# Four attention stages on one core: balanced seats for masked outputs, first heads' rows stored ahead, constants issued later, fills in two halves

## What is computed

```python
x = x + masked_attention(ln(x))    # 16 heads of 8; softmax over keys k >= query q
x = x + ffn0(ln(x))                # one of 8 weight matrices, chosen by argmax
x = x + radial_attention(ln(x))    # exp(-sigma * |q - k|^2), no softmax
x = x + ffn0(ln(x))
x = x + relative_attention(ln(x))  # scores with a shifted relative term, softmax
x = x + ffn1(ln(x))
x = x + rotary_attention(ln(x))    # rotary positions on q and k, softmax
x = x + ffn1(ln(x))
```

## Time and profile before

| | us |
|---|---|
| median of 3 runs | 2823.63 |
| lowest, highest | 2823.32, 2838.18 |
| the profiled execution | 2820.36 |
| its span in the trace | 2818.6 |
| PE busy in it | 2662.6 (94%) |
| ACT busy | 2103.6 (75%) |
| DVE busy | 2070.0 (73%) |
| POOL busy | 898.3 (32%) |

### The profile page before, as it was taken

How to read it: one execution, slowest core, us unless ns; L and a number is a source line. 1 busy time by engine, 2 the same in 40 slices (tenths; PEclk the granted TensorE clock), 3 DMA queues, 4 the chain that set the end, 5 groups by cost and what they waited for, 6 DMA issues and landing times.

```text
span 2818.6 us, 107129 instructions
## 1 busy us (share of the span) xinstructions
PE 2662.6 (94%) x43752; PEld 1600.2 (57%) x43752; DVE 2070.0 (73%) x5519; ACT 2103.6 (75%) x3769; POOL 898.3 (32%) x1604
## 2 busy tenths in 40 slices
PE   5999999999999999999999999999999999999996
PEld 3666665655555555666666666666644444444444
DVE  6788888722222228888788888878889989999993
ACT  3677776799999996666666666666677878878874
POOL 2212223321303242622541361252135144351321
PEclk7999999999999999999999999999999999999998
DMA  3534232433423342411321241222123123232221
GB/s 113 152 100 118 81 115 80 116 119 113 127 88 121 104 147 57 133 53 57 93 88 50 73 131 50 74 81 70 46 64 107 56 71 98 66 98 68 68 72 32
DMA packets 197218, 250.16 MB, mean 89 GB/s; under 512 B 48292, under 2 KB 113124, under 8 KB 196728
## 3 DMA queue, kind: packets, MB, share of 16 engines
q1 hardware_dynamic: 195288, 241.21, 28.9%
q10 hardware_dynamic: 1440, 2.10, 0.2%
HBM read 132.89 MB, written 100.07 MB: 83 GB/s over the span
## 4 chain that ended last, share of the span: by engine, by line
PE 69%; DVE 20%; issue 5%; ACT 2%; DMA 1%; SPq 1%; POOL 0%; ACTq 0%; DVEq 0%; POOLq 0%
PE ppv L1010 29%; DVE mx L1311 14%; PE ring L867 6%; PE ring L917 6%; PE ring L852 5%; PE ring L878 4%; PE ring L950 3%; PE pm L1050 2%; DVE seen L1295 2%; DVE seen L1306 1%; ACT probs L1167 1%; PE ring L966 1%; PE pm L1035 1%; PE pm L1113 1%; PE pm L1104 1%
## 5 line engine op out<-in xcount | busy, mean ns | idle before, releaser
L1167 ACT ACTIVATE probs<-ring 128x512 f32<-128x512 f32 (+1 forms) x3280 | 1970.1, 682 | 647.0 <-PE ring L867 316.0
L1311 DVE TENSOR_REDUCE mx<-ring 128x1 f32<-128x512 f32 (+2 forms) x2112 | 1284.9, 651 | 226.6 <-PE ring L917 89.3
L1010 PE MATMUL ppv<-probs,values 128*32 128x128 f32 x30208 | 1147.3, 278 | 7.5 <-POOL probs L1590 3.1
L1010 PEld LDWEIGHTS ppv<-probs,values 128*32 128x32 f32 x30208 | 793.1, 109 | 320.1 <-issue 162.9
L1306 DVE CUSTOM_DVE_ANT_0 seen<-ring,low_seen 128x512 f32<-128x512 f32 x576 | 392.9, 682 | 71.8 <-PE ring L917 71.5
L924 PE MATMUL ring<-kst,qst 48*128 48x512 bf16 (+1 forms) x1060 | 361.6, 390 | 34.8 <-DMA kst<-records_k 17.4
L878 PE MATMUL ring<-qst,kst 51*128 51x512 bf16 (+2 forms) x1092 | 345.5, 384 | 4.5 <-ACT probs L1167 3.6
L1560 POOL CAST mparts<-mall 128x8 bf16<-128x8 f32 x192 | 37.0, 193 | 827.6 <-DVE mall L1329 700.8
L917 PE MATMUL ring<-kst,qst 112*128 112x512 bf16 (+3 forms) x768 | 251.5, 328 | 11.8 <-DVE mx L1295 6.7
L1590 POOL TENSOR_SCALAR_AFFINE_SELECT probs<-probs 128x512 f32<-128x512 f32 x128 | 81.6, 638 | 564.0 <-ACT probs L1167 351.3
L867 PE MATMUL ring<-qst,kst 115*128 115x512 bf16 (+3 forms) x768 | 250.9, 327 | 0.0
(11 more groups left out here) (170 smaller groups left out, 3001.9 us busy)
## 6 DMA issues: line engine op xcount, KB each, us to landing
qst<-records_q SPq DMA_DIRECT2D x448, 96.0 KB
heads_out<-osb SPq DMA_DIRECT2D x256, 128.0 KB, 2.0
kst<-records_k SPq DMA_DIRECT2D x320, 96.0 KB
records_k<-parts SPq DMA_DIRECT2D x96, 256.0 KB, 3.2
records_q<-parts SPq DMA_DIRECT2D x90, 256.0 KB, 3.4
kst<-records_k SPq DMA_DIRECT2D x128, 102.0 KB
oT<-heads_out SPq DMA_DIRECT2D x60, 128.0 KB, 2.7
proj<-proj SPq DMA_DIRECT2D x96, 64.0 KB, 2.0
```

What stands on the lines that cost most here:

```text
L1010: mm = pe.matmul(ppv[32 * g:32 * g + 32, c:c + P], values[:, (n // H) % 2, v:v + 32], src[:, at * P:(at + 1) * P], start=u == 0 and qt < 4 ...
L1167: nc.scalar.activation(probs_of(rd.n, u), src, ACT.Exp, scale=1.0 if rd.s == RBF else SCALE).then_inc(s_exp, 1)
L1311: ins = dve.tensor_reduce(mx[:, slot, to:to + 1], bank[:, at * P:(at + nt) * P], AX.X, ALU.max)
```

## The change

It has four parts.

1. **Seats.** A function `seat` gives each query tile its column tile. In the masked stage the tiles 4 to 7 are seated in reverse order, 3 to 0, instead of 0 to 3. In `KQ_UNITS[MASKED]` the single tiles (4, 4) and (0, 0) change places between units 3 and 8. The output projection reads `oT` by the same function.
2. **First heads ahead.** The rows of the first `EARLY = 4` heads are stored first, on a semaphore of their own (`s_r0`), and head 0's load waits for these only. The rows of the other 12 are stored by SP after the loads of heads 0 to 2, and by ACT after the small operations of the operator choice.
3. **Constants.** Fourteen constants move to ACT's queue, behind the arrival of the first rows of `x`. SP's `others()` begins in round 3 instead of 1 and issues one transfer every four ticks instead of two; the constants of the last two stages come last and have a semaphore `s_c2`, which PE, ACT, DVE and POOL wait for before round `REL_WORK` = 96, in the middle of the radial stage. The memset of `values` moves from DVE to POOL. SP's rows of ones of the radial stage are issued one by one in `others()`.
4. **Halves.** Where fills are 6 ticks apart (radial and rotary intervals, but not the last radial one), a fill other than `nm` and `zs` is cut in two: the second half (`rest`) is due one tick after the first, and the copy (`take`) and what follows from it one tick later than before. A fill of 512 columns becomes two matmuls of 256 columns, one of four matmuls or transposes becomes two and two.

```diff
+EARLY = 4
 KQ_UNITS = {
-    MASKED: [[(7, 0, 4, 0)], [(7, 4, 4, 0)], [(6, 0, 4, 0)], [(6, 4, 3, 0), (4, 4, 1, 3)], [(5, 0, 4, 0)],
-             [(5, 4, 2, 0), (1, 0, 2, 2)], [(4, 0, 4, 0)], [(3, 0, 4, 0)], [(2, 0, 3, 0), (0, 0, 1, 3)]],
+    MASKED: [[(7, 0, 4, 0)], [(7, 4, 4, 0)], [(6, 0, 4, 0)], [(6, 4, 3, 0), (0, 0, 1, 3)], [(5, 0, 4, 0)],
+             [(5, 4, 2, 0), (1, 0, 2, 2)], [(4, 0, 4, 0)], [(3, 0, 4, 0)], [(2, 0, 3, 0), (4, 4, 1, 3)]],
...
+def seat(s, qt):
+    g = 3 - qt % 4 if s == MASKED and qt >= 4 else qt % 4
+    return g, qt // 4 * P
...
         self.at[("fill", *name)] = tick
-        self.at[("take", *name)] = tick + 1
+        last = tick + (self.apart > 3 and name[2] not in ("nm", "zs"))
+        self.at[("rest", *name)] = last
+        self.at[("take", *name)] = last + 1
         self.free = tick + self.apart
-        return tick + 1
+        return last + 1
...
+        NC_ACT = 16 * 14
+        REL_WORK = (REL * B - 2) * H
...
-                if n % H == 0:
+                if n == 0:
+                    sp.wait_ge(s_r0, 16 * STORES[0])
+                elif n == EARLY or n % H == 0:
                     sp.wait_ge(s_rec, records_to(n // H))
...
-                            if i or g == 0:
+                            if i:
                                 sp.dma_start(dst[lo:lo + H, e * D:(e + 1) * D], parts[:, part, which[e]]).then_inc(s_rec, 16)
+                            elif g == 0:
+                                sp.dma_start(dst[0:EARLY, e * D:(e + 1) * D], parts[0:EARLY * D, part, which[e]]).then_inc(s_r0, 16)
...
-                tick = ROUNDS[1].tick
+                tick = ROUNDS[3].tick
...
-                    tick += 2
+                    tick += 4
...
             for n in range(3):
                 load(n)
+            for e in range(6):
+                sp.dma_start(records_k[EARLY:H, e * D:(e + 1) * D], parts[EARLY * D:P, 0, KPARTS6[e]]).then_inc(s_rec, 16)
...
-                    g, c = qt % 4, qt // 4 * P
+                    g, c = seat(rd.s, qt)
...
                     for n in range(4):
+                        if n == 2:
+                            yield AT["rest", j, i, t, h]
                         mm = pe.transpose(bank[:, n * P:(n + 1) * P], xn[:, 4 * h + n], ident[:, :])
...
+                            whole = AT["rest", *name[1:]] == AT[name]
+                            for c in range(0, HALF, HALF if whole else HALF // 2):
+                                if c:
+                                    yield AT["rest", *name[1:]]
+                                mm = pe.matmul(bank_of(name)[:, c:c + (HALF if whole else HALF // 2)], w, ...)
+                            mm.then_inc(s_pf, 1)
...
                         for t in range(4):
-                            q = (2 * t + h) * P
+                            if t == 2:
+                                yield AT["rest", *name[1:]]
+                            g, c = seat(s, 4 * h + t)
+                            q = 2 * P * g + c
...
             for rd in ROUNDS.values():
                 if rd.n == H:
                     pe.wait_ge(s_c1, NC1[0])
+                    pe.wait_ge(s_c3, NC_ACT)
+                if rd.n == REL_WORK:
+                    pe.wait_ge(s_c2, NC2[0])
...
                         for e in range(6):
-                            act.dma_start(records_q[0:H, e * D:(e + 1) * D], parts[:, 1, QPARTS6[e]]).then_inc(s_rec, 16)
+                            act.dma_start(records_q[0:EARLY, e * D:(e + 1) * D], parts[0:EARLY * D, 1, QPARTS6[e]]).then_inc(s_r0, 16)
...
+            act.wait_ge(s_x[0], 16)
+            for dst, src in [...14 constants...]:
+                act.dma_start(dst, src).then_inc(s_c3, 16)
             act.wait_ge(s_c0, NC0[0])
...
+            for e in range(6):
+                act.dma_start(records_q[EARLY:H, e * D:(e + 1) * D], parts[EARLY * D:P, 1, QPARTS6[e]]).then_inc(s_rec, 16)
...
-                        dve.memset(values[:, :, :], 1.0).then_inc(s_dset, 1)
...
             pool.memset(qst[0][:, :, :], 0.0).then_inc(s_set, 1)
+            pool.memset(values[:, :, :], 1.0).then_inc(s_vset, 1)
```

More of the change, by code:

```diff
@@ L335, in idle @@
             self.free = tick
-            at["take", *name] = tick
+            at["rest", *name] = at["take", *name] = tick
         for t in range(NT + 1):
@@ L509, in build @@
         s_half = sem("s_half")
+        s_vset = sem("s_vset")
+        s_r0 = sem("s_r0")
+        s_c2 = sem("s_c2")
+        s_c3 = sem("s_c3")
         s_cm = sem("s_cm")
@@ L573, in build, with rowb @@
         SETS = 3
-        NCM = [0]
+        NC_ACT = 16 * 14
+        NCM, NC2 = [0], [0]
+        REL_WORK = (REL * B - 2) * H
+        def rowb(v, n=P):
+            return v.rearrange("(o c) -> o c", o=1).to_broadcast([n, v.shape[0]])
         def soft_before(f):
@@ L584, in const0, with const2 @@
                 NC0[0] += 16
+            def const2(dst, src):
+                sp.dma_start(dst, src).then_inc(s_c2, 16)
+                NC2[0] += 16
             def constm(dst, src):
@@ L596, in const1 @@
                 NC1[0] += 16
-            def rowb(v, n=P):
-                return v.rearrange("(o c) -> o c", o=1).to_broadcast([n, v.shape[0]])
             def load_x(b):
@@ L607, in const_rows @@
                 for slot in range(SLOTS):
-                    if s == RBF:
-                        for c in (0, ROW):
-                            e = c + BASE
-                            sp.dma_start(keys[e + 3:e + 6, slot], k["ones3"].bitcast(BF16)).then_inc(s_kc[s], 16)
-                            sp.dma_start(qs[e:e + 3, slot], k["ones3"].bitcast(BF16)).then_inc(s_kc[s], 16)
-                    else:
-                        sp.dma_start(keys[ROW + BASE:ROW + BASE + 3, slot], k["minus3"].bitcast(BF16)).then_inc(s_kc[s], 16)
+                    sp.dma_start(keys[ROW + BASE:ROW + BASE + 3, slot], k["minus3"].bitcast(BF16)).then_inc(s_kc[s], 16)
                     if s == REL:
@@ L772, in others @@
                     yield later()
-                    const1(dst, src)
-                yield later()
-                const_rows(RBF)
-                assert tick < ROUNDS[H - 1].tick
+                    const2(dst, src)
+                assert tick < ROUNDS[REL_WORK - H].tick
             load_x(0)
@@ L1008, in take_values @@
                     if rd.s == MASKED:
-                        last = u == 7 and qt == 3 or u == 8 and (kt, qt) in ((0, 0), (2, 1), (2, 2))
+                        last = final
                     mm = pe.matmul(ppv[32 * g:32 * g + 32, c:c + P], values[:, (n // H) % 2, v:v + 32],
@@ L1264, in _ @@
             nc.scalar.activation(pick[:, 8, 0:1], pick[:, 7, 0:1], ACT.Ln).then_inc(s_ac, 1)
+            for e in range(6):
+                act.dma_start(records_q[EARLY:H, e * D:(e + 1) * D], parts[EARLY * D:P, 1, QPARTS6[e]]).then_inc(s_rec, 16)
             for rd in ROUNDS.values():
+                if rd.n == REL_WORK:
+                    act.wait_ge(s_c2, NC2[0])
                 for u in range(rd.slots):
@@ L1534, in _ @@
             for rd in ROUNDS.values():
+                if rd.n == REL_WORK:
+                    dve.wait_ge(s_c2, NC2[0])
                 for u in range(rd.slots):
@@ L1777, in _ @@
             pool.wait_ge(s_set, SETS)
-            pool.wait_ge(s_dset, 3)
+            pool.wait_ge(s_dset, 2)
             for rd in ROUNDS.values():
                 m = rd.n + 1
+                if rd.n == REL_WORK:
+                    pool.wait_ge(s_c2, NC2[0])
                 for u in range(rd.slots):
```

50 lines of the change are left out of this document (35 added, 15 removed).

## The result

The changed kernel takes 2808.51 us in the median of 7 runs (2797.18 to 2812.5), the kernel before beside it 2823.63 (2822.39 to 2839.46, 7 runs): ratio 0.9923, interval [0.9896, 0.9951]. The forecast was 2798.5 with a range of 2772 to 2814 (2788 to 2810 for my own account without the rivals). The time lies in both, in the narrower one by 1.5 us, but only 15 of the 25 us came. The profiled execution has a span of 2810.1 us against 2818.6.

The account below looks back on a forecast made before the run. PE was taken as the bound, with DVE right behind it in undisturbed masked heads. Terms −22.8 − 5.2 − 7.5 + 10.4 = −25.1 us took the median of 2823.63 to 2798.5 us, range 2772 to 2814.

Parts of the forecast that it names:

- seats: Masked stage: three per column tile in each group of twelve products shortens heads, 22.8 us less, between 8 and 40.
- early stores: Start: storing four heads' rows first lets head 0 load earlier, 5.2 us less, with 2 and 6.5 as ends.
- constants: Masked stage: spreading constants removes waits for `mrow` around 110 to 150 us, net 7.5 us less, between 3 and 9.
- halves: Radial and rotary fills: cutting costs 0.22 and 0.12 us per close fill, net 10.4 us more, between −15 and +26.
- So 0.24 each: Masked stage: each of 26 undisturbed heads gains only DVE's idle 0.24 us before the next head, 6.2 us together.
- heads at 6.4 us would refute VectorE's part: Masked stage test: undisturbed heads forecast at 6.77 us; 6.4 us would refute DVE's part in setting the pace.
- So they are covered: Start: ACT's six late stores, 5.6 us of its queue, are hidden because its first exponential of scores starts in round 0.
- no wait over 2 us: Masked stage test: no `mrow` wait over 2 us around 110 to 150 us, perhaps one in the second interval.
- rival of hidden weight loads and returned idle time: Radial and rotary fills: halves cost nothing or pay back, −10 to −15 us, time 2775 us; chance 0.20.
- PE sets the pace in every masked head: Masked stage rival: the balanced seats give 40 us instead of 22.8, time 2781 us; chance 0.07.
- DVE hides most: Masked stage rival: DVE's work hides most of the seats' gain, leaving 8 us, time 2813 us; chance 0.15.
- slower: Radial and rotary rival: each half starves DVE and ACT anew, 64 us more, time 2852 us; chance 0.04.

Follow-up runs that it names:

- e1: The kernel before with the balanced seats and nothing else; 2806.04 us, ratio 0.9912.
- e4: The kernel before with the constants moved and spread, old seats, whole fills, all sixteen heads' rows stored at once; 2817.68 us, ratio 0.9961.
- e2: The kernel before with fills in two halves and nothing else; 2845.29 us, ratio 1.0053.
- e12: The whole change measured again, unaltered, on another chip; 2805.04 us, ratio 0.9933.
- e7: The kernel before with the new seats but without the exchange of (4,4) and (0,0); a single execution, 2825.69 us.
- e6: The change without the halves, with ScalarE's late stores issued only after the loads of heads 0 to 2 landed; 2796.8 us, ratio 0.9883.
- e9: The kernel of e6 with a masked head's first group of products cut, eight at unit 5 and four at unit 6; 2803.44 us, ratio 0.9916.
- e11: The kernel of e6 measured again, unaltered, beside e9 on one chip; 2807.11 us, ratio 0.9927.
- e10: The kernel before with halves alone, as e2, but the second half two ticks behind the first; a single execution, 2849.97 us.
- e3: The whole change without its halves, so with whole fills; 2797.03 us, ratio 0.9890.

## Why the prediction was right, and where it was not

| term | forecast | measured |
|---|---|---|
| seats | −22.8 | −22.4 in e1, with 10.3 us more at 1.2 GHz than before |
| early stores | −5.2 | −1.0 to −1.1 |
| constants | −7.5 | −9.5, +2.4 in the second interval; e4's masked stage −2.6, with 6.9 us more at 1.2 GHz |
| halves | +10.4 | +12: radial 5.3, rotary 6.7 (e2 against e1) |
| clock | none | +9 in the profile of the change |

The profiled execution was forecast at 2795.3 us and took 2812.4, 17 more: 9 of the clock, 4 of the early stores, 2 of the halves and 1 of the relative stage (988.9 for 987.8) are named; the last us isn't. At equal clock (e12, above) the forecast missed by some 6 us, which is about what start, halves and relative stage lost.

**Seats.** The price per product on the fullest tile, 0.21, was right (e7: 0.20), and the sum was right, but by luck and not by its own steps. "So 0.24 each" for undisturbed heads failed: it was 0.55, because part of VectorE's waiting for TensorE lay inside the merged row of five maxima and between it and the small row before. The statement that heads at 6.4 us would refute VectorE's part applies: TensorE was the pace there too, for all but 0.08 of the 0.63. The error was made good by the others: 14 heads with fills, not 20, gained 0.55 on average and not 0.63; 12 others 0.24 and not 0.4; six heads in which a transfer was the pace gave 0.3 together, and three lost 2.2. Where nothing disturbs, seats and constants together are as forecast: e6 and the kernel before, both with 6.8 us at 1.2 GHz, differ by 30.1 us in the masked stage; −22.8 − 7.5 = −30.3 was the sum. That too is partly luck: by e1 and e4, each with its surplus at 1.2 GHz counted at 0.3 to 0.4, the seats gave some 26 and the constants some 5 (estimates).

**Early stores.** This step failed. I priced a store's issue by the 0.34 us of an unhurried `heads_out` store; six early ones took 4.04 us on SyncE (0.67 each) and 5.51 on ScalarE (0.92 each). Their landing took 3.80 us, nearer the old 4.66 than my 2.6. The load began at 34.95 us and not at 31.3. "So they are covered", said of ScalarE's late stores, was wrong as well: they ran beside the first loads and cost some 0.9 us up to the first score matmul (e6, e9 and e11).

**Constants.** The first interval gave what was said (9.5 for 9.0), and the waits of the second took back 0.8 in e4 and 1.6 in the change, for 1 to 2. What e4's masked stage lost beyond that stands where the clock fell. The forecast of no wait over 2 us was just missed: the chain shows 2.07 and 2.21 us; the third row is the one that was expected in the second interval.

```profile
114.97 2.07 DMA qst<-mrow
128.76 2.21 DMA qst<-mrow
224.26 2.82 DMA qst<-mrow
```

**Halves.** Right in mechanism and nearly in size. Price per fill, spacing (4.70; 6.01 for a forecast of 6.03) and the placing in e10 all came out. The rival of hidden weight loads and returned idle time is refuted: VectorE's waits didn't shrink (48.3 us in e1, 49.4 in e2). A half costs 0.64 us behind products where the whole fill took 1.06: half of the columns take 0.42 us, so 0.22 of a fill does not shrink with them, for a forecast of 0.21. The rule of the Trainium skill (TensorEngine Tiling (Array Packing), Key Properties) that a change of tiling mode drains the engine fits that but isn't singled out by it, since the weight load can be part of the 0.22; the one on overlapped weight loads (TensorE: Matmul & The Clock Gate, Step-by-step) did not make the cut free here.

**Clock.** With the 4 us of the start it is what made the forecast of the profiled execution too low. The other rivals: "PE sets the pace in every masked head" was right on the mechanism for undisturbed heads and wrong on the sum; "DVE hides most" and "slower" are refuted.

**The better version.** Without the halves: 0.9890 [0.9871, 0.9909] in e3, and with the loads ahead of the late stores 0.9883 [0.9865, 0.9902] and 0.9927 [0.9912, 0.9942] in two measurements, against 0.9923 [0.9896, 0.9951] and 0.9933 [0.991, 0.9956] of the change. The ratios alone overlap; the stages say 12 us. The executions with a mean granted clock of 0.985 agree: 2799.62 to 2804.56 us with the halves (five executions of the change), 2788.51 and 2788.17 without them (e3, e6), though on different chips. What stays open is why the clock falls in one execution of a kernel at one of its places and not in the next.

## What to carry to other kernels

A merged row of a timeline can hold waits: compare its length with the same operations where nothing can hold them up before you call an engine the bound. Price a cut by what stands on both sides of each piece, and if the pieces touch already, don't cut. Judge changes of half a per cent by stages with equal time at the lower clock, or by executions with equal mean clock, and not by one ratio.

## What the runs showed that I had not expected

- One kernel measured twice gave 0.9883 [0.9865, 0.9902] and 0.9927 [0.9912, 0.9942].
- A stretch of 23.9 us at 1.2 GHz near the end of the radial stage, in five of the profiles (e1, e2, e6, e7, e11) and not in the others, costs 10 us (518.3 against 508.3). In e6, windows (the last three numbers: the clock's share, DMA, GB/s):

```profile
1000.00:1017.00 17.00, 15.62 (x317) 9.03 (x309) 2.85 (x7) 15.09 (x17) 0.00 (x0) 1.00 0.37 111
1017.00:1041.00 24.00, 24.00 (x177) 8.35 (x165) 11.21 (x32) 8.25 (x14) 0.00 (x0) 0.50 0.07 20
```

- The issue of a transfer has no fixed price. A `heads_out` store costs SyncE 0.34 us; six stores of rows of 64 KB cost 0.67 each on SyncE and 0.92 on ScalarE, six of 256 KB 0.97 and 1.25. A load costs 0.42 in a row of loads (e6) and up to 1.56 beside ScalarE's stores. How much of a store's price is its shape and how much the other queue isn't separated.
